# Graph attention passes: where the requests for the softmax sums stand in GpSimd's queue, and how many row batches are asked for a stage earlier

## The reference

```python
h = x @ W
a_s = h @ att_s
a_d = h @ att_d
a_e = ea @ We @ att_e
alpha = jax.nn.leaky_relu(a_s[src] + a_d[dst] + a_e, NEG_SLOPE)
m = jax.ops.segment_max(alpha, dst, num_segments=n)
ex = jnp.exp(alpha - m[dst])
w = ex / jax.ops.segment_sum(ex, dst, num_segments=n)[dst]
return jax.ops.segment_sum(w[:, None] * h[src], dst, num_segments=n) + b
```

## Time and profile before

| | us |
|---|---|
| three runs, median | 1869.95 |
| profiled execution, its own time | 1871.19 |
| its span, first to last instruction | 1869.3 |
| mean granted clock of TensorE | 0.89 |
| busy in the span: PE / DVE / ACT / POOL | 1563.2 / 1479.7 / 1148.4 / 937.0 |
| row requests of both passes, line 1410, x320 | 327.7 busy |
| requests for the sums, line 1523, x50 | 52.6 busy |

### The profile page before, as it was taken

The page is one execution under the profiler, slowest core; times in us unless marked ns, Lnnn a source line. Parts: engine busy times, 40 slices in busy tenths (PEclk is TensorE's granted clock), DMA queues, the critical chain, the costliest instruction groups (busy, mean ns, idle before and its releaser), DMA issues. The chain is left out here.

```text
span 1869.3 us, 43539 instructions
## 1 busy us (share of the span) xinstructions
PE 1563.2 (84%) x13220; PEld 1350.2 (72%) x13220; DVE 1479.7 (79%) x4411; ACT 1148.4 (61%) x2906; POOL 937.0 (50%) x940
## 2 busy tenths in 40 slices
PE   6699999999999846999674899884659989479996
PEld 5488888888888733555573798784649978379995
DVE  5688888888888688999556998756689977668797
ACT  2577677777777537677310998753059976366572
POOL 4777777777777230000054777755567777300000
PEclk9799999999999967999865899996669999689897
DMA  6888888888888300232273211114621111346561
GB/s 199 246 260 247 244 253 264 256 264 256 252 251 262 115 5 36 95 128 116 101 214 74 62 40 42 42 33 126 149 57 44 41 42 42 124 151 243 200 243 37
DMA packets 148928, 273.55 MB, mean 146 GB/s; under 512 B 28039, under 2 KB 88909, under 8 KB 146436
## 3 DMA queue, kind: packets, MB, share of 16 engines
q1 hardware_dynamic: 110430, 192.44, 31.8%
q0 software_dynamic: 33408, 75.68, 15.1%
q10 hardware_dynamic: 4854, 2.55, 0.6%
HBM read 225.06 MB, written 45.51 MB: 145 GB/s over the span
## 5 line engine op out<-in xcount | busy, mean ns | idle before, releaser
L1002 POOL DMA_INDIRECT gated_rows<-p_tab,src_idx x416 | 434.9, 1045 | 152.0 <-issue 121.2
L1410 POOL DMA_INDIRECT cur<-table,src_idx x240 | 247.0, 1029 | 95.0 <-issue 54.5
L1119 ACT ACTIVATE gated_sig<-gated_pre 128x512 f32<-128x512 f32 x208 | 131.4, 632 | 153.6 <-DVE gated_pre L1207 139.8
L1622 PE MATMUL bank<-attention_counts,h_sb 128*128 128x260 f32 (+1 forms) x900 | 216.4, 364 | 0.0
L1043 PE MATMUL bank<-gated_wide_q,gated_comb 128*128 128x256 f32 x832 | 216.0, 382 | 0.0
L2335 PE MATMUL bank<-mean_wide,mean_xs 128*128 128x416 f32 (+2 forms) x900 | 182.3, 360 | 35.1 <-DVE mean_xs L2451 33.0
L1207 DVE TENSOR_TENSOR gated_pre<-bank,gated_rows 128x512 f32<-128x512 f32 x208 | 142.8, 687 | 77.2 <-PE bank L1043 76.6
L2335 PEld LDWEIGHTS bank<-mean_wide,mean_xs 128*128 128x128 f32 x900 | 165.0, 206 | 38.3 <-ACT mean_wide L2293 33.3
L1550 ACT ACTIVATE attention_lo<-attention_plain,w_left 128x128 fp32r<-128x128 bf16 x512 | 177.3, 398 | 14.1 <-DVE attention_plain L1671 13.7
L1571 ACT COPY attention_counts<-bank 128x475 f32 (+1 forms) x256 | 143.8, 562 | 63.0 <-PE bank L1610 59.5
L1605 PE MATMUL bank<-attention_wide_a,attention_lo 128*128 128x300 f32 x512 | 157.5, 391 | 18.7 <-ACT attention_lo L1550 9.6
(11 more groups left out here) (452 smaller groups left out, 4114.6 us busy)
## 6 DMA issues: line engine op xcount, KB each, us to landing
counts<-count_tabs SPq DMA_DIRECT2D x16, 2675.0 KB, 9.4
h_sb<-in_edge_attr_dram SPq DMA_DIRECT2D x51, 512.0 KB
count_tabs<-mean_counts SPq DMA_DIRECT2D x40, 535.0 KB, 2.8
gated_relr<-rel_rows SPq DMA_DIRECT2D x104, 128.0 KB
gated_ids<-id_rows SPq DMA_DIRECT2D x26, 512.0 KB
gated_wide_q<-q_tab SPq DMA_DIRECT2D x208, 64.0 KB
attend_hot_lo<-low_hots SPq DMA_DIRECT2D x52, 256.0 KB, 4.1
gated_ea<-in_edge_attr_dram SPq DMA_DIRECT2D x51, 256.0 KB
```

Of the source, the lines that this page charges most:

```text
L1002: pool.indirect_dma_start(out=rows[:, q % TICKS, c, :], out_offset=None, in_=p_tab, in_offset=bass.IndirectOffsetOnAxis(ap=src_idx[:, b, j ...
L1119: act.activation(flat(sig[:, q % 4, :, :]), flat(pre[:, q % 2, :, :]), ACT.Sigmoid).then_inc(sig_ready, 1)
L1410: pool.indirect_dma_start(out=ring_row(n, j), out_offset=None, in_=table, in_offset=bass.IndirectOffsetOnAxis(ap=src_idx[:, gathered_batch ...
L1622: mm = pe.matmul(BANKS_D[k % 2][:, 0:width], h_sb[:, m, :], counts[:, home(first), m, at:at + width], start=(m == 0), stop=(m == NT - 1), ...
```

## The change

In `attention_pass` the branch in the loop that put one request for the sums behind each of 25 row batches is gone. The wait for `aux_stored` and all 25 requests now stand behind the loop, that is, behind the last row request of batch 39. `EARLY` goes from 6 to 8: the logits stage asks for all eight places of the ring, and the loop in the pass begins with batch 8. Nothing else is changed.

```diff
-    RING, EARLY = 8, 6
+    RING, EARLY = 8, 8
...
-            AUX_FROM = NGB // 3
...
-                        if n == AUX_FROM:
-                            pool.wait_ge(aux_stored, 16)
-                        if 0 <= n - AUX_FROM < NT:
-                            k = n - AUX_FROM
-                            pool.indirect_dma_start(out=aux_n[:, k, :], out_offset=None, in_=aux_rows,
-                                                    in_offset=bass.IndirectOffsetOnAxis(ap=seg_last[:, k:k + 1], axis=0)).then_inc(aux_in, 16)
+                    pool.wait_ge(aux_stored, 16)
+                    for k in range(NT):
+                        pool.indirect_dma_start(out=aux_n[:, k, :], out_offset=None, in_=aux_rows,
+                                                in_offset=bass.IndirectOffsetOnAxis(ap=seg_last[:, k:k + 1], axis=0)).then_inc(aux_in, 16)
                     pool.wait_ge(summed, NGB)
                     pool.wait_ge(aux_in, 16 * NT)
```

## The result

The changed kernel takes 1.0028 times the time of before (95% interval 1.0015 to 1.0041): 1873.6 us against 1870.4 in the medians of twelve runs each, by the ratio some 5 us slower (2.8 to 7.7). Forecast were 1855 us and a range of 1846 to 1867. Disturbed runs are left out of the ratio.

A forecast was written before the change was run, and what follows sets the result against it. Late rows, at POOL's request rate, cost TensorE 17.3 and 17.0 us in the two passes. Per pass -11.1 + 4.9 - 1.4 = -7.6, together -15.2: 1871.19 to 1856.0 profiled, 1855 on the runs' scale; range 1846 to 1867.

The forecast's parts named there:

- Requests for the sums out of the loop: In the passes: no sum waits for rows any more, TensorE's way gets shorter by 17.3 and 17.0 us.
- POOL, with 5.0 us of slack, becomes the last to arrive: Logits stage's end: eight more requests make POOL last, so each pass begins 4.9 us later.
- zero as the other end of the delay: Start of each pass: the least delay allowed from eight more logits-stage requests, against 4.9 us forecast.
- Nothing but its landing and the end of the block is behind it: End of each pass: 3.98 us from last request to next stage in place of 15.07, saving 11.1 us.
- The chain of requests: POOL's 153 requests from batch 8 on: closer spacing of the sums' requests saves 1.4 us a pass.
- two more batches ahead buy little: Logits stage: asking for eight batches moves batch 8 by the same 4.9 us, at best 4.
- The sum: Each pass by POOL's way: -11.1 + 4.9 - 1.4 = -7.6 us, together -15.2.
- the first: Rival, chance 0.15: stage boundary does not wait for POOL, or POOL is quicker; -25 us or 1845.5, near 1846.
- Late landing: Rival, chance 0.11: sums' last landing at the pass's end takes 9.8 us, not 2.4; 1869.6, no change.
- POOL's rate: Rival, chance 0.09: POOL's requests in the passes slow to 1.458 us each; +17.6 us in all, 1887.5.

The follow-up runs named there:

- e2: Kernel before with only EARLY raised from 6 to 8, requests for the sums left in the loop: 1.0083 of the time of before, 15.5 us slower.
- e11: Changed kernel plus a drain behind batch 0 in GpSimd's logits-stage list: last request's end to next stage 3.07 and 3.13 us, 5.04 without.
- e12: Sums last, EARLY 6, VectorE waiting for their landing, plus a GpSimd drain before the sums' requests: end of pass 3.03 and 3.01 us, 6.3 without.
- e5: Kernel before with EARLY = 4, fourth batch asked for only after VectorE's last copy: 3.74 us from last request's end to next stage.
- e3: Changed kernel with GpSimd memset marks around a wait for the last batch's landing: next stage 5.05 us behind the second mark in the logits stage.
- e4: Kernel before with EARLY = 4, GpSimd waiting for VectorE's last copy, then a memset: 1.0153 of the time of before; 3.74 us from memset to next stage.

## Why the prediction was wrong, by its own steps

*Requests for the sums out of the loop: right.* No row wait is left, and TensorE's way got shorter by 17.7 and 16.7 us (17.3 and 17.0 forecast).

*"POOL, with 5.0 us of slack, becomes the last to arrive": this step failed in its size.* That POOL arrives last was right. The slack was read as the time from the end of POOL's last request (1022.08) to VectorE's end (1027.09). POOL was not idle in it: its drain and the meeting behind it took 4.39 us for 49 requests, and 4.4 of the 5.4 us up to the pass were used. 5.37 - 4.39 leaves 0.98 us, the lead over VectorE that the drains' own records show. The eight requests add 8 x 1.25 and 8 x 0.082, 10.66 us; less 0.98 that is 9.68 us, and 9.65 was measured in both layers. The prediction said that no run before showed POOL arriving last, and so kept zero as the other end of the delay; it put the drain at nothing without a reason and gave no end above 4.9.

*"Nothing but its landing and the end of the block is behind it", 3.98 us: failed for the same reason.* 1.58 us is what VectorE needs to leave the pass. GpSimd's way is 9.79 and 9.11 us; by the records of its sequencer that is 2.9 and 2.6 until the sums have landed, 1.1 and 0.8 for the branch, 5.4 for the drain and 0.3 for the meeting. Before, the 15.07 us behind the last request hid this as well.

*The chain of requests: right in the mean alone.* For the 153 requests from batch 8 on 1.4 us less were forecast; the last one started 4.0 us earlier in the first pass, counted from its start, and 0.8 later in the second. That their mean, 1.6, is near the forecast is luck. That two more batches ahead buy little was right: the passes of e2 gained 0.9 and 0.4 us.

*The sum:* -15.2 forecast, 9.5 for the two late starts (9.65 - 4.9 each), 10.9 for the two tails (5.8 and 5.1), -0.3 for the chains: +4.9, and +5.2 (2.8 to 7.7) was measured.

*The rivals:* none had this cost. In the first, -25 gives 1845 on the runs' scale, not the 1846 written, which is the profiled execution's; nothing hangs on it. Late landing came near the time (1869.6) by luck, for another reason, and its place is refuted: the sums' landing stayed at a median of 2.4 us and a longest of 3.4. With it goes the consequence drawn there from the Trainium skill ("DMA: Bandwidth & Descriptors", Specifications, on transfers under 512 bytes): 25 requests of 16-byte pieces in a row did not pile up. POOL's rate did not fall: 1.33 and 1.35 us from batch 8 on. That the boundary waits for POOL is shown by e2.

## What to carry to other kernels

The time from an engine's last row to a meeting of all engines is slack only if something showed the engine idle in it. A drain has no row in these views, so bound its price on both sides, and read it from its record in the trace or from a run in which that engine arrives last. In this kernel GpSimd paid for its gathers once more at the end of each of the two stages, and its list has to end that much before the other engines are done; a drain put in earlier only moved a part of that (e11, e12). And where two edits go together, price each alone: here the first gives 11 us, the second takes 15.

## What the runs showed of the hardware that was not expected

In the logits stages GpSimd's drain behind indirect DMAs of 128 pieces took 3.4 us after 41 of them, 4.1 after 49, 4.7 after 57 and 6.75 after 82: 0.08 us each and under 0.1, whether the last was just issued (e5), had landed (e3), or was 14.5 us old (e4); with 0.3 us for the meeting that is 3.73 to 7.1 from GpSimd's last instruction to the next stage. A memset in its place started within 0.01 us of the request's end. A drain in between resets the count, but for about five (e11) to seven (e12). In the passes with the sums last it was 4.0 us after 136 requests, 5.4 after 153 and 6.0 to 6.1 after 161: the same 0.08 us each, as if some 88 had been paid for; why stays open, and so does the 8.7 and 9.4 us of the drain in the middle of e11.
